# A transformer block's warm-up reordered: keys' rotary products ahead of low parts, modulation vectors in banks of their own, gate matrices loaded in the prologue, third queries' casts behind the first rows

## The reference

```python
ga = (2 * (ga >= 0) - 1) * jnp.maximum(jnp.abs(ga), 0.25)   # gb likewise
h = _layernorm(x) * (1 + ca) + sa
x = x + ga * _L0_attn_ref(h, Wq, Wk, Wv, Wo)
h = _layernorm(x) * (1 + cb) + sb
x = x + gb * _L0_ffn_ref(h, w_gate_up, w_proj)
```

## Time and profile before

| | |
|---|---|
| time of 3 runs, median | 1859.02 us |
| lowest, highest | 1857.18, 1862.01 us |
| profiled execution, time | 1858.29 us |
| profiled execution, span | 1856.3 us |
| TensorE busy, share of the span | 1747.3 us, 94% |
| VectorE, ScalarE, GpSimd busy | 1259.0, 1147.6, 964.8 us |
| granted TensorE clock, mean | 0.987 |

### The profile page before, as it was taken

The page is one execution under the profiler, slowest core; times in us unless marked ns, Lnnn a source line. Parts: engine busy times, 40 slices in busy tenths (PEclk is TensorE's granted clock), DMA queues, the critical chain, the costliest instruction groups (busy, mean ns, idle before and its releaser), DMA issues. The chain is left out here.

```text
span 1856.3 us, 28089 instructions
## 1 busy us (share of the span) xinstructions
PE 1747.3 (94%) x9505; PEld 1394.7 (75%) x9505; DVE 1259.0 (68%) x2078; ACT 1147.6 (62%) x2315; POOL 964.8 (52%) x773
## 2 busy tenths in 40 slices
PE   6899999999999999999999999996999999999998
PEld 3577787777777777778777777774788778888886
DVE  5787887788788778788778878884333355545343
ACT  4578787777777777877777777784322354323322
POOL 1256667666667666666766666753000035444454
PEclk9999999999999999999999999998999999999999
DMA  6433444344344344344434434425655400101000
GB/s 229 121 94 103 120 102 124 100 109 121 88 131 114 86 123 112 92 117 108 121 103 108 125 83 134 119 82 163 208 179 177 134 29 1 52 1 51 1 29 23
DMA packets 174969, 190.95 MB, mean 103 GB/s; under 512 B 31456, under 2 KB 117736, under 8 KB 174832
## 3 DMA queue, kind: packets, MB, share of 16 engines
q1 hardware_dynamic: 137840, 140.99, 26.7%
q10 hardware_dynamic: 36992, 48.25, 9.4%
HBM read 86.12 MB, written 31.74 MB: 63 GB/s over the span
## 5 line engine op out<-in xcount | busy, mean ns | idle before, releaser
L926 DVE TENSOR_TENSOR p_lo<-ps_b,p_hi 128x512 fp32r<-128x512 f32 x576 | 395.3, 686 | 194.7 <-ACT p_hi L829 190.8
L844 ACT ACTIVATE p<-ps_b,negm 128x640 f32<-128x640 f32 (+7 forms) x512 | 381.9, 749 | 111.4 <-DVE negm L934 108.5
L829 ACT CAST p_hi<-ps_b 128x512 fp32r<-128x512 f32 x576 | 337.0, 588 | 156.9 <-PE ps_b L748 154.2
L934 DVE TENSOR_REDUCE negm<-ps_b 128x1 f32<-128x640 f32 (+7 forms) x512 | 375.8, 744 | 34.1 <-PE ps_b L738 33.4
L748 PE MATMUL ps_b<-ident,p 128*128 128x128 f32 x2304 | 350.3, 275 | 3.1 <-DVE p_lo L926 2.1
L736 PE MATMUL ps_b<-k_hh,q_hl 128*128 128x512 f32 (+3 forms) x768 | 270.1, 352 | 37.0 <-ACT p L844 36.0
L762 PE MATMUL ps_b<-p_hi,v_hl 128*128 128x512 f32 x576 | 276.9, 481 | 16.4 <-ACT o_sb L837 16.1
L748 PEld LDWEIGHTS ps_b<-ident,p 128*128 128x128 f32 x2304 | 259.0, 141 | 37.3 <-DVE p_lo L926 5.1
L737 PE MATMUL ps_b<-k_l,q_hl 128*128 128x512 f32 (+3 forms) x768 | 256.1, 346 | 0.0
L763 PE MATMUL ps_b<-p_lo,v_hl 128*128 128x512 f32 x576 | 227.6, 395 | 0.0
L736 PEld LDWEIGHTS ps_b<-k_hh,q_hl 128*128 128x128 f32 x768 | 145.1, 189 | 87.4 <-ACT p L844 54.7
(11 more groups left out here) (156 smaller groups left out, 3202.6 us busy)
## 6 DMA issues: line engine op xcount, KB each, us to landing
rot_x<-rot_s SPq DMA_DIRECT2D x320, 64.0 KB, 2.0
q_hl<-rot_s SPq DMA_DIRECT2D x128, 128.0 KB, 2.5
q_hl<-rot_x SPq DMA_DIRECT2D x128, 128.0 KB, 2.5
rd_all<-reciprocals SPq DMA_DIRECT2D x128, 128.0 KB, 3.0
o_low<-o_sb ACTq DMA_DIRECT2D x128, 128.0 KB, 2.4
attention_out<-o_sb SPq DMA_DIRECT2D x128, 128.0 KB, 2.5
o_raw<-attention_out SPq DMA_DIRECT2D x32, 512.0 KB, 4.9
wf<-in_L_ffn_w_gate_up ACTq DMA_DIRECT2D x32, 256.0 KB, 3.0
```

The costliest lines, as they stand in the source:

```text
L829: act.copy(p_hi[:, T % P_RING, :], ps[:, T_BANK + T % 2, :]).then_inc(phi_ready, 1)
L844: act.activation(p_32[:, parity, h, column * P:column * P + nk], s, ACT.Exp, bias=negm[:, k:k + 1], scale=1.0, accum_out=den[:, parity, k: ...
L926: dve.tensor_tensor(p_lo[:, T % P_RING, :], ps[:, T_BANK + T % 2, :], p_hi[:, T % P_RING, :].bitcast(F32), ALU.subtract).then_inc(plo_read ...
L934: dve.tensor_reduce(negm[:, k:k + 1], s, AX.X, ALU.max, negate=True).then_inc(max_ready, 1)
```

## The change

- VectorE makes the rotary products of use 6 before the low parts 2 and 3 of chunk 1 (both now in step 36); statistics of chunk 2 move from step 36 to 37, the root from 41 to 38.
- The shift and scale products of the second stage go to PSUM banks 2 and 3 instead of 4 and 5, and the first no longer waits for the modulation of chunk 1. The second is cut in two halves, in steps 41 and 43, around the turn of the values in step 42. The first transposes of chunk 2 wait until both results are copied.
- The gate matrices (two DMAs of 1 MB) are issued in the prologue, ahead of the last chunk of x, and not in step 50. The prologue's normalised rows move out of p_32 to make room.
- The two constants' casts move from step 52 to 58. A small Exp on ScalarE in step 59 is added.
- For uses 11 and 12 in the warm-up, ScalarE's cast and GpSimd's subtraction move from start + 8 to start + 12 (steps 62 and 67 become 66 and 71), and the placing from start + 10 to start + 12 (64 and 69 become 66 and 71).

```diff
--- before.py
+++ after.py
@@ -99,22 +99,17 @@
         flat = p_32[:].rearrange("p a h c -> p (a h c)")
         size = CT * 2 * E
         self.late = [flat[:, at:at + size].rearrange("p (k v e) -> p k v e", k=CT, v=2) for at in (0, 2 * GQ * 9 * P - size)]
-        self.flat = flat
         self.late_in, self.gate_in = sem("late_in"), sem("gate_in")
         self.late_done, self.late_rows, self.late_turned, self.modT_late = [sem(n) for n in (
             "late_mm", "late_rows", "late_turned", "modT_late")]
         self.gate_copied, self.gate_link, self.gates_done, self.gates_out = [sem(n) for n in ("gcopied", "glink", "gates", "gout")]
 
-    def rows_at(self, n):
-        size = 4 * E
-        return self.flat[:, (2 + n) * size:(3 + n) * size].rearrange("p (t e) -> p t e", t=4)
-
     def load_gates(self, sp, wmod):
         for v in range(2):
             sp.dma_start(self.late[1][:, :, v, :], mod_columns(wmod)[:, :, GATE[v], :]).then_inc(self.gate_in, 16)
 
-    def product(self, pe, out, wm, v):
-        for kc in range(CT):
+    def product(self, pe, out, wm, v, pieces=range(CT)):
+        for kc in pieces:
             i = pe.matmul(out, self.cs[:].rearrange("p (b k) -> p k b", b=B)[:, kc, :], wm[:, kc, v, :],
                           start=(kc == 0), stop=(kc == CT - 1))
         return i
@@ -151,7 +146,7 @@
         sb = lambda n, s: ctx.enter_context(nc.sbuf_tensor(n, s, F32))
         self.xt = sb("xt_l", [P, 2, 4, E])
         self.xn = sb("xn_l", [P, 2 * P_RING, 512])[:, 0:4, :]
-        self.h32 = [sb("h32_l%d" % n, [P, 2, 512]) for n in range(2)]
+        self.h32 = sb("h32_l", [P, CT, 512])
 
     def statistics(self, dve, n, xt):
         chain = Chain(dve, self.link, n * LINKS)
@@ -213,7 +208,7 @@
         rows_sb = sb("m_rows", [B * CT, 2, E], F32)
         m_rows, c_rows, cs_rows = rows_sb[0:B], rows_sb[:, 0, 0:P], rows_sb[:, 1, 0:P]
         x_rows = sb("x_rows", [P, 2, 4, E], F32)
-        xt, xn = [x_rows[:, n] for n in range(2)], [vectors.rows_at(n) for n in range(2)]
+        xt, xn = [x_rows[:, n] for n in range(2)], [late.h32, late.xn]
         h32 = sb("h32", [P, CT, 512], F32)
         MOD_BANK, C_BANK = 6, 7
         cs = vectors.cs
@@ -243,6 +238,7 @@
             load_x(2, late.xt[:, 0])
             for v, place in enumerate((SHIFT[1], SCALE[1])):
                 sp.dma_start(vectors.late[0][:, :, v, :], wm_v[:, :, place, :]).then_inc(vectors.late_in, 16)
+            vectors.load_gates(sp, wmod)
             load_x(3, late.xt[:, 1])
 
         @block.scalar
@@ -346,12 +342,14 @@
 NG = UW // QG
 START = 28
 W_HIGH, W_LOW, W_LOAD, WO_LOAD = 28, 29, 2, 4
-LATE_AT, LATE_TURN, LATE_ROWS = (35, 41, 64, 66), 70, (45, 45)
-GATE_LOAD, GATE_STEPS, GATE_STORE = 50, 67, 71
-ROWS_STAT, ROWS_ROOT, ROWS_NORM, ROWS_TURN = (36, 49), (41, 50), (44, 54), (48, 58)
+LATE_AT = ((35, 0, (0, 1, 2, 3)), (41, 1, (0, 1)), (43, 1, (2, 3)), (64, 2, (0, 1, 2, 3)), (66, 3, (0, 1, 2, 3)))
+LATE_BANK, LATE_ROWS, LATE_TURN = (2, 3, T_BANK, T_BANK + 1), (45, 45), 70
+GATE_STEPS, GATE_STORE = 67, 71
+ROWS_STAT, ROWS_ROOT, ROWS_NORM, ROWS_TURN = (37, 49), (38, 50), (44, 54), (48, 58)
 ROWS_MOD = ((28, 29, 30, 31), (49, 50, 51, 51), (59, 60, 61, 62))
-ROWS_LOW = ((31, 32, 33, 34), (55, 55, 56, 56), (59, 60, 61, 62))
-CONSTS_AT, KEYS_AT, QUERY_SWAP = 52, 12, 59
+ROWS_LOW = ((31, 32, 36, 36), (55, 55, 56, 56), (59, 60, 61, 62))
+CONSTS_AT, KEYS_AT, QUERIES_AT, QUERY_SWAP, TABLE_AT = 58, 12, 12, 59, 59
+
 
 
 
@@ -586,7 +584,7 @@
 
         def late_h32(n, k):
 
-            return spare[:, k // 2, k % 2, :] if n == 1 else late.h32[k // 2][:, k % 2, :]
+            return spare[:, k // 2, k % 2, :] if n == 1 else late.h32[:, k, :]
 
 
         @block.sync
@@ -636,13 +634,15 @@
             def step(body, T):
                 places_first = body.before(T, QUERY_SWAP)
                 if places_first:
-                    for g, n, _ in body.uses(T, 10, kinds=("qx", "qy")):
+                    for g, n, _ in body.uses(T, 10, kinds=("qx",)):
                         place(g, n)
                 for g, n, _ in body.uses(T, 5, kinds=("kv", "qx", "qy")):
                     swap(g, n)
                 if not places_first:
-                    for g, n, _ in body.uses(T, 10, kinds=("qx", "qy")):
+                    for g, n, _ in body.uses(T, 10, kinds=("qx",)):
                         place(g, n)
+                for g, n, _ in body.uses(T, QUERIES_AT if body.g < 0 else 10, kinds=("qy",)):
+                    place(g, n)
                 for g, n in body.pairs(T, 2):
                     save_den(g, n)
                 for k in range(2):
@@ -650,9 +650,6 @@
                         spread_den(g, 2 * n + k)
                 for g, n in body.blocks(T, LAG + 5):
                     store(g, n)
-                if body.before(T, GATE_LOAD):
-                    sp.wait_ge(vectors.late_done, 2)
-                    vectors.load_gates(sp, wmod)
                 if body.before(T, GATE_STORE):
                     sp.wait_ge(vectors.gates_done, 1)
                     for v in range(2):
@@ -767,24 +764,26 @@
                 for k in range(CT):
                     if k == 0 or n == 3:
                         pe.wait_ge(late.h_ready, 2 * CT + (k + 1 if n == 3 else 0))
+                    if k == 0 and n == 2:
+                        pe.wait_ge(vectors.late_rows, 2)
                     late.turn(pe, n, k, ps[:, turned_bank(n, k), :], late.xn, ident)
 
-            def late_product(v):
+            def late_product(v, pieces):
                 if v == 0:
                     pe.wait_ge(vectors.late_in, 32)
-                    pe.wait_ge(late.h_ready, 2 * CT)
-                if v >= 2:
+                if v >= 2 and 0 in pieces:
                     pe.wait_ge(vectors.gate_in, 32)
-                    pe.wait_ge(vectors.late_rows, v - 1)
-                vectors.product(pe, ps[0:B, T_BANK + v % 2, :], vectors.late[v // 2], v % 2).then_inc(vectors.late_done, 1)
+                i = vectors.product(pe, ps[0:B, LATE_BANK[v], :], vectors.late[v // 2], v % 2, pieces)
+                if CT - 1 in pieces:
+                    i.then_inc(vectors.late_done, 1)
 
             def step(body, T):
                 for n in (2, 3):
                     if body.before(T, ROWS_TURN[n - 2]):
                         late_turns(n)
-                for v in range(4):
-                    if body.before(T, LATE_AT[v]):
-                        late_product(v)
+                for at, v, pieces in LATE_AT:
+                    if body.before(T, at):
+                        late_product(v, pieces)
                 if body.before(T, LATE_TURN):
                     for v in range(2):
                         pe.wait_ge(vectors.late_rows, v + 1)
@@ -864,10 +863,12 @@
                     act.wait_ge(consts_in, 48)
                     act.copy(ident_b[:], ident[:]).then_inc(consts_ready, 1)
                     act.copy(mask_b[:], mask[:]).then_inc(consts_ready, 1)
+                if body.before(T, TABLE_AT):
+                    act.activation(den[:, 1, :], ident[:, 0:len(ROWS)], ACT.Exp)
                 for v in range(2):
                     if body.before(T, LATE_ROWS[v]):
                         act.wait_ge(vectors.late_done, v + 1)
-                        act.copy(rd_all[0:B, v, :], ps[0:B, T_BANK + v, :]).then_inc(vectors.late_rows, 1)
+                        act.copy(rd_all[0:B, v, :], ps[0:B, LATE_BANK[v], :]).then_inc(vectors.late_rows, 1)
                 if body.before(T, LATE_TURN + 1):
                     act.wait_ge(vectors.late_turned, 2)
                     for v in range(2):
@@ -901,7 +902,7 @@
                     rows_s.await_(act, g, 23 if unit == 0 else (55 if n == X_BODY - 1 else 55 - RB))
                     for rows in half:
                         act.copy(k_hh[unit][rows, kv_cols(part)], rot_c[0:D, part, :]).then_inc(khi_ready, 1)
-                for g, n, _ in body.uses(T, 8, kinds=("qx", "qy")):
+                for g, n, _ in body.uses(T, 8, kinds=("qx",)) + body.uses(T, QUERIES_AT if body.g < 0 else 8, kinds=("qy",)):
                     buf = buf_of(n)
                     buf_sum[buf].await_(act, g, BUF[buf].index(n))
                     act.copy(rot_s[:, buf, :].bitcast(F32R), rot_c[:, buf, :]).then_inc(qhi_ready[buf], 1)
```

## The result

The changed kernel takes 1864.97 us (median of 22 runs, 1855.77 to 1870.5), the kernel before 1859.12 us (22 runs, 1854.51 to 1865.49): a ratio of 1.0027, 95% interval 1.0016 to 1.0037. Run again beside its variants it gave 1862.96 us and 1.0026 (1.0011 to 1.0041). The forecast was 1856 with a range up to 1859.8, so the sign was wrong. The loss is 5.9 us by the medians.

What follows compares the result with a forecast made beforehand. TensorE, busy 94% of the span, was taken as the bound, so only its warm-up idle time could be won. 4.2 − 1.3 = 2.9 us off 1858.3 gives 1855.4, as a median 1856; range 1852.5 to 1859.8.

Steps and rivals of the forecast that it cites:

- the same work in the same order: From first score to first turn: two products of 3.6 us and the score rows, 18.08 us, put as unchanged.
- The term of 1.3 us: After step 71: a later swap of use 13 makes ScalarE wait 1.3 us, returned as TensorE idle time; bounds 0 to 2.6.
- The term of 4.2 us: At the first score row: start at 66.3 us instead of 70.50, a gain of 4.2 us.
- On ScalarE the cast of use 10 ends at 58.7: Steps 49 to 63: constants, modulations and table load follow this cast, and ScalarE ends at 65.9 in place of 69.98.
- a cost that I put at nothing: VectorE and GpSimd overlap: only VectorE's loss was priced, 1.1 us at chunk 2's normalisation; no delay of GpSimd's addition.
- 0.9 were allowed: Before the first score: moving the table load from 74.58 into ScalarE's earlier chain costs up to 0.9 us.
- a first score after 68: Sign of being wrong: first score expected at 66 to 67 us; after 68 would mean the lock, a backlog or the clock.
- The queue chain after step 71: SyncE's queue: cast, GpSimd, four placings, eight gate stores, then the swap of use 13 issued at 95.9, GpSimd adding at 98.5.
- 3.0 us were counted for this chain: Swap of use 10 to GpSimd's addition: no longer queued behind the gate load, 3.0 us leave, on top of 2.9.
- The drain of 1.38 us: Table load on ScalarE: by the skill 1.28 us plus this drain, making the gain 2.8 us; the trace was used instead.
- Rival 2: SyncE's queue in step 71: swap 3 us later takes the whole gain, 3 us more gives 1862; chance 0.07.
- Rival 4: No gain: lowered clock on the 3.6 us products or one more time, 1.5 us each, plus key cast; 1859; chance 0.10.

Runs made afterwards that it cites:

- e6: The changed kernel unaltered, run once more on the chip of its variants: 1862.96 us, ratio 1.0026 to the kernel before.
- e1: Changed kernel with casts, subtractions and placings of uses 11 and 12 back in their old steps: 1857.83 us, ratio 1.0000 to the kernel before.
- e9: Changed kernel with only the placing of use 12 put behind the gate stores and the swap of use 13 on SyncE's queue: 1858.08 us, ratio 0.9994.
- e4: Kernel before with only the casts, subtractions and placings of uses 11 and 12 moved to steps 66 and 71: 1858.72 us, ratio 1.0007.
- e3: Kernel before with only the gate matrices loaded in the prologue and its normalised rows outside p_32: 1857.59 us, ratio 1.0004.
- e5: Changed kernel with uses 11 and 12 back in old steps, no small Exp, and constants' casts back in step 52: 1856.81 us, ratio 0.9989.
- e7: As e5, with the two gate products cut in halves and put in steps 47, 54, 59 and 64: 1852.04 us, ratio 0.9966.
- e8: As e5, with the first two low parts of chunk 2 in step 52: 1854.02 us, ratio 0.9979.
- e11: Kernel before with only rotary products first, shift and scale products in banks 2 and 3 and cut, statistics and root moved: 1857.05 us, ratio 0.9987.
- e12: The edits of e7 and e8 together, on e5: 1853.44 us, ratio 0.9965.
- e2: Changed kernel without the small Exp in step 59 and with the constants' casts back in step 52: 1856.70 us, ratio 0.9997.
- e10: Changed kernel with only the gate products moved into TensorE's waits (steps 47, 54, 59, one half in 64): 1853.98 us, ratio 0.9973.

## Why the prediction was wrong

**The steps that failed** are both terms of the sum, 4.2 − 1.3, and a stretch between them that was put at no change. By the second profile (e6), whose first projection runs at full clock as it does before, the gain at the first score is 1.1 us and not 4.2; from there to the first turn 1.65 us are lost, where "the same work in the same order" was to take the same time; and from there to the weights 4.0 us are lost and not 1.3. That is 4.5 us lost where 2.9 were to be won.

**The term of 1.3 us**, "So 1.3 us come back as TensorE's idle time". The mechanism was right and named (cast, GpSimd, placing, gate stores, swap, ScalarE's wait of 1.3 us; measured 1.22, and 1.14 more idle time on TensorE). The price was not: I let an idle time cost its own length. In the changed kernel it is followed by 6.8 us at half the clock, in both profiles, and the stretch to the weights is 4.0 us longer, not 1.1. e1 and e9, which shorten the idle time by two different edits, bring those 4.0 us back. In e4, where the clock stays up, the price is the length.

Over all profiles, the idle time of TensorE behind that exponential and the clock in the microseconds after it stand like this:

| idle time | kernels | lowered clock just after |
|---|---|---|
| 0.86 to 1.35 us | before, e1, e3, e5, e7, e8, e9, e11, e12 | none in nine |
| 2.09 to 2.11 us | changed, e6, e2, e10, e4 | 6.8, 6.8, 3.4, 3.4, 0 us |

It is nearly so before the first score row: where TensorE idled 2.2 to 2.5 us there (changed, e1, e6, e9), the clock fell within 1 us and the stretch to the first turn took 19.7 to 19.8 us; where it idled 0 to 1 us (before, e4, e5, e8, e11), it took 18.0 to 18.1. Two kernels stand apart. e3 has no idle time there, but 3.7 us before use 12 and a clock that is low from there into the score rows; it took 18.4. e2 took 19.7, because its clock fell (81.05) after an idle time of only 1.58 us at 80.39; all other kernels but e7, e10 and e12 have the same idle time and keep their clock. Before the transposes of chunk 2, 2.3 to 2.6 us of idle time (changed, e1, e5, e6, e8, e9, e11) go with transposes of 3.3 to 3.6 us, and where half a gate product fills that time down to 0.3 to 0.5 us (e7, e10, e12), they take 1.94; but they take 1.94 in e4 too, behind 2.26 us. Over the fourteen profiles, from 28 to 160 us, TensorE has 31 idle times of 2 us or more; at 28 of them the clock is low by the end or falls within 1.5 us of it. Of 35 between 1 and 2 us, five are so. The length is a strong sign and not the whole rule.

The mean granted clock of all runs says it without a profile: 0.9844 over 22 runs of the changed kernel, and 0.9854 over 12 more (e6) beside 0.9879 for before on the same chip. The difference of 0.0024 of 1858 us is 4.5 us, nearly the whole 4.65 of e6's loss: what the change won and lost in waits cancels, and what is left is lowered clock. e9 (0.9876, before 0.9877) has none of it. e1 (0.9858, before 0.9873) keeps 2.7 us of it and makes them up in waits.

**The term of 4.2 us** at the first score was too large: the second profile (e6) has 69.37, 1.1 earlier than before, and the first 70.86, where a lowered clock at the start of the first projection costs 1.5 more. The transposes start as forecast (46.46 in e6, forecast 46.7; three GpSimd instructions on one normalisation, as said, 4.96 us for the four in the first profile), and so does use 12 (62.36, forecast 62.0). The step that failed is "On ScalarE the cast of use 10 ends at 58.7": in e6 it ends at 62.0. 1.2 of the 3.3 us come from the transposes, which run at the lowered clock (3.44 us, not 1.94) and so delay use 10. The other 2.1 come from a cost that I put at nothing. I looked at what GpSimd's instructions cost VectorE, and not at the other direction: the earlier start puts VectorE's four subtractions beside GpSimd's addition, which then takes 3.4 to 3.5 us instead of 1.27. e8 shows it by two subtractions less. From the cast on the chain is as long as forecast (7.3 us to the first score), but now it stands alone behind all others, so the load and the constants count in full: from the start of use 12 to the first score it is 7.06 us in e1 and 5.57 in e5, the same kernel without them (use 12 itself starts 1.3 us later in e5's profile, whose first projection ran at the lowered clock). That is 1.5 us, where 0.9 were allowed. TensorE idles 2.4 us before the score, and the second lowered clock follows; in e5 it idles 0.96 us and the clock stays up. The prediction had named a first score after 68 as a sign of being wrong, by the lock, a backlog or the clock; it was the lock and the clock.

**What held.** The queue chain after step 71 holds to 0.2 us: counted from the first turn, the swap of use 13 is issued 7.1 us later (forecast 7.3 us, from 95.9 against a first turn of 88.58 in the old count). The 2 MB of gates moved away are worth nothing alone (e3): the projection of use 12 holds the score. That was not forecast so, as 3.0 us were counted for this chain. The early parts are worth 2.5 us at the first score (e11). The drain of 1.38 us of which the Trainium skill speaks ("ScalarE: Activation LUTs", section "What ACT_TABLE_LOAD costs") is not in this trace: the load at 65.30 takes 1.28 us and is followed by the Exp at 66.59.

**The rivals.** Rival 2 named the right place and asked for 3 us more delay of the swap; the loss came without that delay. Rival 4 had the lowered clock as an accident ("one more time than now, 1.5 us each"); it came in both profiles of the changed kernel, and its stretches are longer. Both should have been one case.

**What stays open.** The rule of the clock: e4 has the same idle time of 2.10 us, and its clock stays up. What differs is what TensorE did ahead of it, and e10, where that was changed, has half the lowered stretch. e2, with half of it too, differs ahead as well. What lets GpSimd's addition get in between the subtractions is open, too: in the five profiles where it does, GpSimd has idled 0.4 to 0.9 us before it, and in the seven where it waits, 2.3 to 3.3 us. No run changes that alone. Why e5, e8 and e11 lie at 1854.0 to 1857.1 with marks within 1.1 us of each other is not resolved by their intervals.

## What to carry to other kernels

Where one engine is busy 94% of the time, an idle time of it that passes about 2 us may cost 2 to 4 us and not its length (in e4 it cost its length); count the waits that a change makes longer, wherever they are, and fill them (e7: 7.2 us of products put into waits, with e12 the best of these versions, 0.34% under the kernel before). When an issue moves on a DMA queue, write down everything it is now ahead of; here four issues in the wrong place cost 5 to 6 us. And when two engines share something, price the collision for both: the single instruction may wait for the other engine's whole row, or get in and make the row longer, and this document has both.

## What the runs showed of the hardware that was not expected

A single GpSimd addition with two SBUF inputs that starts beside four back-to-back VectorE subtractions with two SBUF inputs took 3.2 to 3.5 us instead of 1.27 in five profiles (changed, e1, e5, e6, e9) and 2.22 us beside two (e8): it ended 1.1 us after the row. In five others (e2, e3, e7, e10, and e12 with its row of two), starting as early in the row, it took 1.59 to 1.67 us, and one subtraction took 1.76 us instead of 0.68. Against four VectorE instructions with a scalar operand it got in: in the changed kernel three GpSimd instructions of 1.29 to 1.46 us made these 4.96 us long instead of 1.91, each of them stretching one to 1.5 to 1.7 us (e1, e5 to e10 and e12: 4.7 to 4.9 us). After an idle time of 2.1 us the granted clock of TensorE was 0.52 over the next 6.8 us in one kernel and 1.00 in another.
